# A two-layer masked attention kernel on one core: a new GpSimd order for the adjacency loads, their conversion and the base load, and 20 instead of 16 block moves per step on the sync queue in the last two steps of the first group's row blocks

## What is computed

```python
h = jnp.maximum(_layernorm(x, axis=-1), 0.0)                  # x: 4096 x 256
adj = jnp.maximum(adjacency_matrix, eye)                      # 4096 x 4096, about 0.4% ones
q = jnp.einsum('nd,hdk->hnk', h, Wqs)                         # 8 heads of 64; k and v in the same way
scores = jnp.einsum('hqk,hmk->hqm', q, k) * kd ** (-0.5)
scores = scores + IDENTITY_BIAS * eye - MASK_VAL * (1.0 - adj)
att = jax.nn.softmax(scores, axis=-1)
x = x + jnp.einsum('hqm,hmk,hko->qo', att, v, Wo)
```

## Time and profile before

| | |
|---|---|
| time, median of 3 runs | 2683.47 us (2678.8 to 2686.79) |
| profiled execution, its own time | 2697.21 us |
| its span, first to last instruction | 2695.6 us |
| PE busy | 2628.1 us, 97% |
| DVE busy | 2254.0 us, 84% |
| ACT busy | 1849.3 us, 69% |
| POOL busy | 1282.0 us, 48% |

### The profile page before, as it was taken

The page is one execution under the profiler, slowest core; times in us unless marked ns, Lnnn a source line. Parts: engine busy times, 40 slices in busy tenths (PEclk is TensorE's granted clock), DMA queues, the critical chain, the costliest instruction groups (busy, mean ns, idle before and its releaser), DMA issues.

```text
span 2695.6 us, 58321 instructions
## 1 busy us (share of the span) xinstructions
PE 2628.1 (97%) x17344; PEld 1901.4 (71%) x17344; DVE 2254.0 (84%) x3833; ACT 1849.3 (69%) x3041; POOL 1282.0 (48%) x2424
## 2 busy tenths in 40 slices
PE   8999999999999999999999999999999999999997
PEld 5766767677776767777767777777677777777775
DVE  7888888888888888888848888888888888888885
ACT  4667666677667667677646777777677777777774
POOL 3355655565664555665522444443434444443433
PEclk9999999999999999999999999999999999999999
DMA  6476876676776676776653656565566666565664
GB/s 180 122 172 141 188 179 158 165 178 146 187 183 164 163 168 147 189 184 163 175 155 87 147 148 164 146 161 135 131 149 150 156 149 161 138 148 136 157 144 106
DMA packets 263999, 419.05 MB, mean 155 GB/s; under 512 B 100032, under 2 KB 121024, under 8 KB 259840
## 3 DMA queue, kind: packets, MB, share of 16 engines
q1 hardware_dynamic: 174176, 231.24, 33.4%
q0 software_dynamic: 89760, 187.05, 30.5%
HBM read 136.84 MB, written 46.27 MB: 68 GB/s over the span
## 4 chain that ended last, share of the span: by engine, by line
PE 61%; DMA 10%; SPq 9%; DVE 8%; issue 5%; POOL 5%; DVEq 0%; POOLq 0%; ACT 0%
PE psS L480 23%; PE psO L517 11%; PE psO L503 10%; PE psT L493 10%; SPq L265 9%; DMA S<-S 7%; POOL S L324 4%; DVE S L757 3%; DVE S L778 3%; DMA B<-in_adj 2%; PE psS L434 2%; PE psP L465 1%; DMA rden_scratch<-rden 1%; PE psP L164 1%; PE psP L453 1%
## 5 line engine op out<-in xcount | busy, mean ns | idle before, releaser
L324 POOL DMA_DIRECT2D S<-S x2048 | 1004.5, 499 | 1130.9 <-DVE S L778 1084.4
L757 DVE CUSTOM_DVE_ANT_0 S<-psS,B 128x1024 f32<-128x1024 f32 x1024 | 1228.8, 1219 | 271.4 <-PE psS L480 150.7
L636 ACT ACTIVATE S<-S,negm 128x1024 f32<-128x1024 f32 (+1 forms) x768 | 1095.8, 1428 | 84.9 <-DVE negm L764 84.4
L643 ACT ACTIVATE PT<-psT 128x512 f32<-128x512 f32 x1024 | 594.0, 595 | 261.5 <-PE psT L493 242.4
L480 PE MATMUL psS<-K,QH 128*128 128x512 f32 x2048 | 730.6, 438 | 33.7 <-DVE mx L757 31.3
L480 PE MATMUL psS<-K,QL 128*128 128x512 f32 x2048 | 642.1, 395 | 0.0
L778 DVE STREAM_TRANSPOSE S<-S 128x2048 f32<-128x2048 f32 x256 | 590.4, 2306 | 31.3 <-PE psO L517 27.9
L493 PEld LDWEIGHTS psT<-ident,S 128*128 128x128 f32 x4096 | 480.8, 140 | 186.1 <-issue 73.3
L493 PE MATMUL psT<-ident,S 128*128 128x128 f32 x4096 | 607.0, 276 | 2.9 <-ACT PT L643 2.9
L503 PE MATMUL psO<-PT,V 128*64 128x256 f32 x4096 | 492.1, 382 | 0.0
L517 PE MATMUL psO<-S,V 128*64 128x256 f32 x4096 | 473.7, 384 | 4.0 <-DMA S<-S 4.0
(11 more groups left out here) (51 smaller groups left out, 958.4 us busy)
## 6 DMA issues: line engine op xcount, KB each, us to landing
S<-S SPq DMA_DIRECT2D x2048, 64.0 KB, 3.1
S<-S POOLq DMA_DIRECT2D x2048, 64.0 KB, 2.9
B<-in_adj POOLq DMA_DIRECT2D x128, 256.0 KB, 6.9
bias_scratch<-B SPq DMA_DIRECT2D x32, 1024.0 KB, 6.3
B<-bias_scratch SPq DMA_DIRECT2D x128, 256.0 KB, 5.0
hq<-hT_scratch SPq DMA_DIRECT2D x32, 256.0 KB, 3.7
RB<-rden_scratch SPq DMA_DIRECT2D x128, 64.0 KB, 3.5
S<-in_x SPq DMA_DIRECT2D x8, 512.0 KB, 4.0
```

Of the source, the lines that this page charges most:

```text
L324: pool.dma_start(dst, src).then_inc(late_sent[q][half], 16)
L636: nc.scalar.activation(part, part, ACT.Exp, bias=negm[:, h % 2, q:q + 1], accum_out=sums[:, h % 2, q, e:e + 1]).then_inc(probs_ready, 1)
L643: nc.scalar.activation(PT[:, s % RING, :], psT[s % 2][:, :], ACT.Copy).then_inc(pt_act, 1)
L757: nc.vector.tensor_tensor_reduce(out=part, in0=psS[j % 2][:, :], in1=B[:, q, k * SLOT:(k + 1) * SLOT], scale=SCALE, scalar=LOWEST, op0=ALU ...
```

## The change

There are three edits.

1. In steps 2 and 3 of the first group's row blocks SP issues 10 moves of each tile and POOL 6 (`MORE_SHARE`), 5 and 3 of each half. Everywhere else it stays 8 and 8. The waits for them count accordingly (`sent_by`).
2. POOL's order in step 2 of the first group: after the moves of q = 1 it now issues four adjacency loads (two of q = 0, two of q = 1), then converts two, issues the last two loads, and converts two more. The conversions of the first two slots of q = 1 go to step 3, between the moves of its two tiles.
3. `load_base` goes from step 2 to step 1, right behind `store`, in both groups. The wait for the store, which stood before the base load, stays in step 2 and now raises the semaphore `res_free`, for which VectorE waits before it writes `res` in step 3's `add_heads`.

```diff
+EVEN_SHARE = ((1, 3), (1, 3))
+MORE_SHARE = ((1, 3), (1, 2, 3))
...
+    def share(h):
+        return MORE_SHARE if norm and h >= GROUP // 2 else EVEN_SHARE
+    def sp_moves(h, half):
+        return [((j - d) % QUAD, j) for j in range(2 * half, 2 * half + 2) for d in share(h)[j % 2]]
+    def pool_moves(h, half):
+        return [((j - d) % QUAD, j) for j in range(2 * half, 2 * half + 2) for d in range(QUAD) if d not in share(h)[j % 2]]
+    def sent_by(moves, i, h):
+        per_head = [16 * len(moves(e, 0)) for e in range(GROUP)]
+        return i * sum(per_head) + sum(per_head[:h])
...
+            if adj_rest:
+                for k in range(2):
+                    convert(i + 1, 1, k, own_slot)
             move_late(i, h, 1)
             if adj_step:
                 for k in range(2, SPT):
                     load_adj(i + 1, 0, k)
+                for k in range(2):
+                    load_adj(i + 1, 1, k)
             if prev and h == 1:
                 store(i - 1)
+                load_base(i)
             if prev and h == 2:
                 pool.wait_ge(stored, i * 16)
-                load_base(i)
+                pool.sem_inc(res_free, 1)
             if adj_step:
-                for half_ in range(2):
-                    for k in (2 * half_, 2 * half_ + 1):
-                        convert(i + 1, 0, k, own_slot)
-                    for k in (2 * half_, 2 * half_ + 1):
-                        load_adj(i + 1, 1, k)
                 for k in range(2):
-                    convert(i + 1, 1, k, own_slot)
+                    convert(i + 1, 0, k, own_slot)
+                for k in range(2, SPT):
+                    load_adj(i + 1, 1, k)
+                for k in range(2, SPT):
+                    convert(i + 1, 0, k, own_slot)
...
+            if h == GROUP - 1:
+                dve.wait_ge(res_free, i + START)
```

More of the change, by code:

```diff
@@ L30 @@
 HALVES = 2
-SP_MOVES = [[((j - d) % QUAD, j) for j in range(2 * half, 2 * half + 2) for d in (1, 3)] for half in range(HALVES)]
-POOL_MOVES = [[((j - d) % QUAD, j) for j in range(2 * half, 2 * half + 2) for d in (0, 2)] for half in range(HALVES)]
-MOVED = 16 * len(SP_MOVES[0])
+EVEN_SHARE = ((1, 3), (1, 3))
+MORE_SHARE = ((1, 3), (1, 2, 3))
 OWN_EVERY = SLOT // QW
@@ L94, in group_programs @@
     if not norm:
-        late_used_before, late_moved_before, late_sent_before, slot_masked_before, projected_before, o_summed_before, head_added_before, bias_kept_before, pt_free_before, project_before, next_w_before, next_h_before = before
+        late_used_before, late_moved_before, late_sent_before, late_moved_all, late_sent_all, slot_masked_before, projected_before, o_summed_before, head_added_before, bias_kept_before, pt_free_before, project_before, next_w_before, next_h_before = before
     heads = slice(g * GROUP, (g + 1) * GROUP)
@@ L118, in group_programs @@
     bias_kept = sem(f"bias_kept{g}")
+    res_free = sem(f"res_free{g}")
     (bias_conv, bias_ready, q_proj, q_hi, q_lo, scores_ready, slot_masked, row_ready, probs_ready,
@@ L238, in rows_again @@
                 for half in range(HALVES):
-                    sp.wait_ge(late_moved_before[q][half], MOVED * STEPS)
-                    sp.wait_ge(late_sent_before[q][half], MOVED * STEPS)
+                    sp.wait_ge(late_moved_before[q][half], late_moved_all[half])
+                    sp.wait_ge(late_sent_before[q][half], late_sent_all[half])
             load_weights(Wq, wq_first, wqf_in)
@@ L262, in move_late @@
             for half in range(HALVES):
-                for qi, qj in SP_MOVES[half]:
+                for qi, qj in sp_moves(h, half):
                     src, dst = late_blocks(h, q, qi, qj)
@@ L321, in move_late @@
             for half in range(HALVES):
-                for qi, qj in POOL_MOVES[half]:
+                for qi, qj in pool_moves(h, half):
                     src, dst = late_blocks(h, q, qi, qj)
@@ L356, in constants @@
             pool.wait_ge(consts, 3)
+        pool.sem_inc(res_free, START)
         if norm:
@@ L511, in values_late @@
                     for half in range(HALVES):
-                        pe.wait_ge(late_moved[q][half], count(i, h, MOVED, MOVED))
-                        pe.wait_ge(late_sent[q][half], count(i, h, MOVED, MOVED))
+                        pe.wait_ge(late_moved[q][half], sent_by(sp_moves, i, h + 1))
+                        pe.wait_ge(late_sent[q][half], sent_by(pool_moves, i, h + 1))
             PTL = S[:, h % 2, :, LC:N].rearrange("p q (i m a) -> p m q i a", i=QUAD, a=32)
@@ L752, in mask @@
                 tq, half = staged_in(j)
-                dve.wait_ge(late_moved[tq][half], count(i, h, MOVED, 0))
-                dve.wait_ge(late_sent[tq][half], count(i, h, MOVED, 0))
+                dve.wait_ge(late_moved[tq][half], sent_by(sp_moves, i, h))
+                dve.wait_ge(late_sent[tq][half], sent_by(pool_moves, i, h))
             wait_apart(dve, scores_ready, count(i, h, SLOTS, j + 1), dve_passed)
@@ L882, in group_programs @@
     return ((sync_program, gpsimd_program, tensor_program, scalar_program, vector_program),
-            (late_used, late_moved, late_sent, slot_masked, projected, o_summed, head_added, bias_kept, pt_free,
+            (late_used, late_moved, late_sent, [sent_by(sp_moves, PAIRS, 0)] * HALVES, [sent_by(pool_moves, PAIRS, 0)] * HALVES, slot_masked, projected, o_summed, head_added, bias_kept, pt_free,
              lambda pe: project(pe, PAIRS - 1, GROUP - 1), next_w, next_h))
```

## The result

The changed kernel takes 2711.26 us (median, 2709.07 to 2714.68) against 2685.12 us before (the 2683.47 from which the prediction starts, with a fourth run added): a ratio of 1.0103, interval 1.0082 to 1.0123. It is 26 us slower; 2716 was predicted. The profiled execution of the changed kernel took 2714.68 us, that of before 2697.21, so the two profiles hold only 17.5 us of the 26. The profiled execution of the changed kernel is one of its four timed runs; that of before is none of its four, and lies 10 us above the slowest of them.

The account below looks back on a forecast made before the run. TensorE, busy 97%, was taken as the bound, with late moves already on its path. 15 x (2.6 - 0.3) = 34.5 us minus 2 gave +32 us: 2730 us profiled, 2716 us median, range 2664 to 2740.

Parts of the forecast that it names:

- The place and the sign: First group's step 2: SP already issues last, so its longer row of issues makes the kernel slower; chance 0.57.
- the assumption that the stretch from issue to landing stays: Step 2: slot 7 keeps starting 6.7 us after SP's last issue, so SP's later issue delays it in full.
- The term of 2.6 us: Step 2, per row block: SP's four extra issues delay slot 7 and TensorE by 2.6 us, ends -1.3 and +3.5.
- Step 3: First group's step 3: slot 7 starts at 15.2 instead of 15.56 us after the transposition, a 0.3 us gain.
- POOL's lateness: First group's step 3: POOL about 0.6 us late for its moves instead of 3.3 us.
- The order of the loads: Step 2: loads come earlier, the base load leaves; one against the other counted as nothing.
- The second group: The base load leaves its step 2, at most an eighth of 15.7 us waiting; 2 us gain in all.
- The sum: 15 row blocks x (2.6 - 0.3) = 34.5 us, minus 2 us: +32 us overall.
- A: Rival: waits of steps 2 and 3 vanish as POOL's lateness goes; 2651 us, with half of it 2667; chance 0.17.
- B: Rival: DMA engines limit, whoever issues; step 2 stays, step 3 gains 0.3 us; 2677 to 2691 us; chance 0.15.
- C: Rival: earlier loads delay SP's last moves; step 2 loses 3.5 us, step 3 another 0.5; 2742 us; chance 0.11.
- the packets: Step 2's DMA queues: the skill's whole-packet turns fit 81.8% against 11.0% only if load packets are much longer than moves'.

Follow-up runs that it names:

- e9: The changed kernel with the 10 and 6 share in step 2 only, step 3 back at 8 and 8; 2700.78 us, 1.0008 of before.
- e1: The changed kernel with SP and POOL sharing moves 8 and 8 everywhere, leaving the new order and early base load; 2666.62 us, 0.9946 of before.
- e2: The kernel before with only the 10 and 6 share in steps 2 and 3 of the first group; 2729.80 us, 1.0176 of before.
- e3: The kernel before with only the base load moved from step 2 to step 1, both groups; 2680.12 us, 0.9984 of before.
- e6: The changed kernel, but in step 3 POOL waits for VectorE's product of Oodd and RB before its last two conversions; 2710.96 us, 1.0041 of before.
- e8: e1, but in step 2 of the first group SP issues 6 moves of a tile and POOL 10; 2684.04 us, 0.9938 of before.
- e7: e1, but step 2's first pair of adjacency loads is issued behind the moves of q = 1; 2666.13 us, 0.988 of before.

## Why the prediction was right

**The place and the sign.** Step 2 was named, and SP's longer row of issues as the cause there. The row lasts 13.6 us instead of 11.1 (means of 14 row blocks), 2.5 more as worked out. The last move lands 18.8 us after the transposition instead of 17.2, so only 1.6 of the 2.5 us arrived: the assumption that the stretch from issue to landing stays did not hold. It shrank from 6.1 to 5.2 us. The term of 2.6 us measured 1.57 in the whole change, 1.4 in e9 against e1, 2.4 in e2 against before. An effect that was missed stands beside it: SP's last move of q = 0 is now issued behind POOL's first loads and lands 12.7 us after the transposition instead of 9.4 (means), and slot 5 waits for it, 2.74 us in the row block shown. Slot 7 was to wait 3 to 4 us and waits 1.1 (mean), as before: it starts 0.3 us after the last landing, but slots 5 and 6 had waited ahead of it. VectorE's waits for moves in the first group rose to 72.1 us, not to about 95, and the distance from step 1 to 2 to 23.05 us, not to about 24.

**Step 3.** The term was -0.3 us and the trace has -0.42, but by cancellation of two others. POOL's lateness went as predicted, to 1.0 us, and was worth 1.17 us (e1 against before; 0.89 against e3), more than the 0.69 us taken as its limit from one row block. SP's 20 moves, which were to eat it up, did no harm (e6). The collision of conversions with VectorE's product, which the prediction did not have, took 0.75 us of it.

**The order of the loads** was counted as nothing in step 2, and e1 bears this out (+0.22 us against before, +0.29 against e3).

**The second group** is 6.1 us shorter in the profiled execution, 2 were expected. VectorE's waits for moves in it fell from 15.7 to 5.8 us, more than the eighth that the prediction allowed, and this goes with the move of the base load: they are 7.5 us or less in every trace that has it, and 13.7 in e2, which has not. But little of it is time: e2's second group is as short as the others, and e3, with the base load alone, was 2 us faster altogether. The rest of the 6.1 may be single disturbances of before's profile, and is open.

**The sum.** The prediction had 34.5 us in the row blocks. Between the two profiles it is 15.3 us there (2.7 in the first row block, 0.9 in each of the others), plus the 7.7 us at the end of the first group, which no rival had, less the 6.1 us of the second group and 0.4 us elsewhere: 16.5 us, the difference of the spans. So by the profiles the row blocks have less than half of what was predicted. That the time rose by 26 us while the profiles differ by 17.5 lies on the side of before: its profiled execution took 12 us more than its median, the changed kernel's 3.4 us. By the medians, edit by edit: the new order and the base load gave 15.5 us (e1), where the prediction had 15 x 0.3 + 2 = 6.5; the share on top of them cost 44.6 us (2711.26 against 2666.62), where it had 15 x 2.6 = 39. Between these two profiles it is 35 us in the row blocks and 8.3 us at the end of the first group. So the total was met to 5 us by luck: the gain was too small by 9 us, the cost by 6 us, since a step 2 term that was too large stood against two costs that were missing, and step 3 was right for the wrong reason.

**The rivals.** A (faster) has its half in e1, 2666.62 us: POOL's lateness in step 3 goes, as A said, but the wait of step 2 stays (21.70). In the changed kernel the stretch from SP's last issue to slot 7 fell from 6.4 to 5.4 us (means), not under the 4.1 that A needed. B (the DMA engines are the limit, no matter who issues) holds in e8 and not in e9. C (the earlier loads cost 3.5 us in step 2) is refuted by e1, 0.22 us. By the rule of the Trainium skill quoted for B, page "DMA: Bandwidth & Descriptors", section "Issuing engines are not separate DMA queues", the split saves issue time only; the traces add that it can also cost it: in steps 2 and 3 SP spends 0.63 to 0.70 us on a move (20 in 12.65 and 13.92 us) and POOL 0.50 (6 in 2.98). As to the packets, which the prediction left at a condition: the earlier trace rows give 201 packets to q0 in 81.8% of the engines' time and 100 to q1 in 11.0%, so over these 4 us of 16 engines a packet of the loads' queue took 0.26 us and one of SP's 0.07 us. They are much longer, and q0 also had twice as many; whether the profile's packets are those of the rule, no run shows.

## What to carry over

When two queues share a row of transfers, look which of them lands last before shifting work, and look at what stands between the transfers in the queues: here moving two loads was worth as much in the distance of step 2 (1.50 us, e7) as the shift cost there (1.43 us, e9), though 0.86 us of it was lost again in step 3. An engine that is relieved comes earlier to whatever it does next; ask what that will meet. And end a change at its borders too: the last step before another stage has other neighbours than the steady loop.

## What was not expected of the hardware

A VectorE product of two operands in SBUF took up to 2.8 us instead of 0.42 beside GpSimd's conversions of 1.04 us, while masks with one operand in PSUM kept their 1.22 us. Between 1183 and 1187 us, with loads and moves in both queues, the share of the sync queue's moves was 11%; with the loads behind the moves (e7) a move landed in 3.0 instead of 5.4 us. The kernel before took 2682 us on one chip and 2699 to 2701 us in two sets on another; by the distances from step 0 to 1 about 5 us of it lie there, and the rest is open.
